# RWKV low-rank mixes on 32 of the 128 rows of TensorE each

## The chip, the cores and the metric

The kernel runs on one core of one Trainium2 chip. The metric is the device time of one execution in microseconds (us), the median of several runs. The engines are TensorE (PE for its matmuls, PEld for its weight loads), VectorE (DVE), ScalarE (ACT), GpSimd (POOL) and the queue that starts DMAs (SP). PSUM is the memory that TensorE writes; it has eight banks of 512 float32 columns on 128 partitions.

## What is computed

The program is a stack of eight residual layers over an input of 32 sequences of 256 tokens with 128 features. Only the first layer, an RWKV-like mixer, is touched by the change. Its beginning, cut from the reference:

```python
shifted = jnp.pad(x, ((0, 0), (1, 0), (0, 0)))[:, :T]
delta = shifted - x
low = jnp.tanh((x + delta * mu_x) @ W_x1).reshape(B, T, 5, PROJ_LR)   # PROJ_LR = 32
mus = jnp.einsum('blnr,dnr->blnd', low, W_x2) + x_bias
xr, xw, xk, xv, xg = [x + delta * mus[:, :, i] for i in range(5)]
r = (xr @ W_r)...; w = (jnp.tanh(xw @ W_w1) @ W_w2 + b_w2)...; k = (xk @ W_k)...
v = (xv @ W_v)...; g = xg @ W_g
```

After that comes a scan over time (S = exp(-exp(w)) * S + k v, per head), a normalisation per head, a gate and an output projection. The five slices of `mus` are the five mixes. Each sums over 32 numbers only.

## The kernel before, in words

The function `stage_rwkv` (from L316) works on 16 groups p of 512 tokens (two sequences). Each group's activations lie with the features on the 128 partitions and the 512 tokens in the free dimension. Everything is float32, and every float32 matmul is recorded as two passes, each with its own weight load.

The low rank of a group is made by two products (`low_rank`, L648 to L653). The first puts columns 0 to 127 of the 160 low-rank columns on the partitions of `low[:, 0]`, the second puts columns 32 to 159 on those of `low[:, 1]`. So the 32 numbers of mix i lie on partitions 32i to 32i+31 of `low[:, 0]` for i = 0 to 3, and on partitions 96 to 127 of `low[:, 1]` for i = 4. The weights `a_wx2` of mix i are laid out on 128 partitions, with zeros on the 96 that do not belong to it. The product of mix i (L565) contracts all 128 partitions; the zeros cancel the rest.

The five products are issued in the order i = 1, 3, 2, 4, 0 (`ORDER`), as j = 0 to 4. They go to PSUM banks 0, 1, 2, 3 and again 0 (`BANK`). So j = 4 must wait until VectorE has read j = 0 out of bank 0 (the wait on `dm_done`). VectorE reads each product with one instruction, `mix_out` (L388), which computes (product + bias) * delta; POOL adds x to three of the five (`add_x`, L516).

Each engine has a list of work written by hand, a loop over g that mixes steps of different groups. The order within one turn is:

- PE: `values(g)` (L553, four products), `mixes(g+1)` (L565, five), `out(g-2)` (L630), `heads(g-1)` (L640, L644), `turn_in(g+2)` (L572, which waits for the residual of VectorE, L456), `decay_low`, `plain_value`, `key`, `decay`, `gate` (L578 to L608), `bonus(g)` (L615), `receptance(g+1)` (L621, L623), `turn_back(g-1)` (L589), `low_rank(g+2)` (L651, L653).
- DVE: `gated(g-2)` (L451), four `outer(g)` (L396), `mix_out` 0 and 1, `scan` 0 (L404), `bonus_key`, `mix_out` 2 to 4, `scan` 1, `residual(g-2)` (L456), `scan` 2 and 3, `variance`, `mix_in(g+2)` (L382), `normalise(g-1)`, `moments(g+3)`, `gate(g+1)`, `bonus_value(g)` (L417).
- ACT: `square`, `evac(g+2)` (L700), `decay_low`, `plain_value`, `root(g-1)` (L691), `key`, `decay`, `gate` (L732), `receptance` (L738), `layernorm(g+3)` (L745), `affine(g-1)` (L715), `low_rank(g+2)` (L757).
- POOL: `add_x`, `read` (L523), `difference` (L511) and `inverse` (L504).

The first turns (g = -3 to -1) fill this pipeline and the last empty it. The two matmuls `decay` (L604) and `bonus` (L615) contract 64 partitions only. In a later layer the product L1142 takes 128 partitions in, but gives 32 columns only, and four heads are put on the four strips of 32 PSUM partitions.

Of the kernel before, what the change touches and what calls it, by code (L numbers as in the profile page):

```python
# [81 lines left out]
def at_least(eng, sem, v):  # L82

    if not (isinstance(v, int) and v <= 0):
        eng.wait_ge(sem, v)
# [193 lines left out]
def stage_rwkv(nc, k, tag, w, x_in, arrive, loads):  # L279
# [5 lines left out]
    with ExitStack() as ctx:  # L285
# [12 lines left out]
        low = sb("low", [P, 2, GW])  # L298
# [38 lines left out]
        at = {name: bank[:, b, :] for name, b in BANK.items()}  # L337
# [206 lines left out]
        def _(pe):  # L544
# [10 lines left out]
            def mixes(p, j):  # L555
                i = ORDER[j]
                if j == 0:
                    pe.wait_ge(s["low_out"], 2 * p + 2)
                elif j == 1:
                    at_least(pe, s["vv_out"], p)  # L560
                elif j == 2:
                    at_least(pe, s["gg_done"], p)
                elif j == 4:
                    pe.wait_ge(s["dm_done"], 5 * p + 1)
                nc.tensor.matmul(at[f"m{j}"], lhsT=w["a_wx2"][:, i, :], rhs=low[:, i // 4, :], start=True, stop=True)\  # L565
                    .then_inc(s["mus_done"], 1)

            def turn_in(p):
# [86 lines left out]
            for g in range(-3, NG + 2):  # L655
                if has(g):
                    for v in range(VQ):
                        values(g, v)
                if has(g + 1):
                    for j in range(5):  # L660
                        mixes(g + 1, j)
                if has(g - 2):
                    out(g - 2)
                if has(g - 1):
                    heads(g - 1)
                if has(g + 2):
                    turn_in(g + 2)
                if has(g + 1):
                    decay_low(g + 1)
                    plain_value(g + 1)  # L670
                    key(g + 1)
                    decay(g + 1)
                    gate(g + 1)
                if has(g):
                    bonus(g)
                if has(g + 1):
                    receptance(g + 1)
                if has(g - 1):
                    turn_back(g - 1)
                if has(g + 2):  # L680
                    low_rank(g + 2)
# [1960 lines left out]
```

## Time and profile before

| What | Value |
|---|---|
| Median of 3 runs | 3591.35 us (3590.38 to 3592.12) |
| The profiled execution's own time | 3593.28 us |
| Its span, first to last instruction | 3591.5 us |
| PE busy (matmuls) | 3117.2 us, 87% |
| PE weight loads | 2057.7 us, 57% |
| DVE busy | 2379.6 us, 66% |
| ACT busy | 1703.2 us, 47% |
| POOL busy | 1203.7 us, 34% |
| Mean granted TensorE clock | 0.905 of full speed |
| Part of the RWKV layer in the span | about 17 to 488 us |

The busy time of PE is that of modelled records: matmuls are pipelined, and a record is longer than the time in which its engine can start the next one. The start of one group to the start of the next is the better measure. A wait in square brackets is the idle time of that engine just before the instruction, with what ended it.

### The profile page before, as it was taken

The page shows a single profiled execution, that of the slowest core. Times are in us where ns is not written, and L with a number is a line of the kernel's source. Part 1 is how long each engine was busy: PE and PEld are TensorE (multiplying, and loading weights), DVE is VectorE, ACT ScalarE, POOL GpSimd, SP SyncE. Part 2 cuts the span into 40 slices and gives each one's busy share as a digit, 9 for nine tenths or more (in the row PEclk, how much of TensorE's full clock was granted, in tenths as well). Part 3 has the DMA queues.
Part 4 walks back from the last instruction along what each step waited for, and adds up shares of the span by engine and source line. Part 5 has one row for each costly group of instructions (what it writes and reads, how often), then busy time and mean ns, then how long its engine had stood idle before and what let it go on. Part 6 is the DMA issues. An engine that isn't in the chain of part 4 may idle for free. (4 is left out here: it accounts for less than half of the span.)

```text
span 3591.5 us, 49433 instructions
## 1 busy us (share of the span) xinstructions
PE 3117.2 (87%) x16500; PEld 2057.7 (57%) x16500; DVE 2379.6 (66%) x5557; ACT 1703.2 (47%) x3659; POOL 1203.7 (34%) x1204
## 2 busy tenths in 40 slices
PE   6999975999872999997589996888989999999989
PEld 2455564888631444444478885677735555555557
DVE  4888875444595777775744445003579999999964
ACT  2443422333231899997133331212446666666644
POOL 3444420000132777775100001001224444444432
PEclk9999967999986999999599995557989999999999
DMA  3000011110032110111111100000000000000001
GB/s 110 1 1 1 1 46 59 39 41 25 26 111 74 29 29 26 29 30 48 53 69 36 45 1 1 0 0 26 1 1 1 1 1 1 1 1 1 1 6 43
DMA packets 106556, 91.24 MB, mean 25 GB/s; under 512 B 15501, under 2 KB 96147, under 8 KB 104000
## 3 DMA queue, kind: packets, MB, share of 16 engines
q1 hardware_dynamic: 104928, 87.25, 7.6%
q8 instruction: 135, 2.21, 0.3%
q14 instruction: 117, 0.96, 0.1%
q10 hardware_dynamic: 1376, 0.82, 0.1%
HBM read 57.60 MB, written 30.15 MB: 24 GB/s over the span
## 5 line engine op out<-in xcount | busy, mean ns | idle before, releaser
L2328 ACT ACTIVATE m_x_hT<-m_x_hid,wm_b 128x260 f32<-128x260 f32 x512 | 242.8, 478 | 433.3 <-PE m_x_hid L2250 433.3
L1326 POOL TENSOR_TENSOR c_tE<-c_tE,c_tDm 128x256 f32<-128x256 f32 x512 | 372.8, 729 | 139.0 <-ACT c_tE L1286 122.3
L1209 DVE TENSOR_REDUCE c_tM<-c_tpa 128x2 f32<-128x512 f32 x512 | 330.0, 681 | 131.2 <-PE c_tpa L1111 130.3
L1286 ACT ACTIVATE c_tE<-c_tpb 128x512 f32<-128x512 f32 x512 | 310.1, 607 | 43.0 <-PE c_tpb L1128 43.0
L2250 PE MATMUL m_x_hid<-m_x_xg,wm_w 128*128 128x260 f32 x1024 | 305.9, 385 | 8.8 <-ACT m_x_hT L2328 5.3
L2258 PE MATMUL m_x_yp<-m_x_hT,wm_w 128*128 128x260 f32 x1024 | 300.6, 383 | 0.0
L1662 POOL TENSOR_TENSOR b_wkv<-b_at,b_rec 128x512 f32<-128x512 f32 x128 | 163.3, 1275 | 306.0 <-DVE b_rec L1598 306.0
L1111 PE MATMUL c_tpa<-c_tK,c_Qm 96*128 96x256 f16 x1024 | 205.1, 283 | 48.8 <-DMA c_Qm<-aug_d 35.6
L79 POOL TENSOR_TENSOR rstd<-vareps,neg_half 128x4 f32<-128x4 f32 x80 | 86.4, 1080 | 460.0 <-DVE vareps L68 460.0
L2175 DVE TENSOR_SCALAR m_x_yT<-m_x_yp,wm_b 128x260 f32<-128x260 f32 x128 | 62.5, 489 | 253.4 <-PE m_x_yp L2258 253.4
L1128 PE MATMUL c_tpb<-c_Qm,c_tK 101*128 101x256 f16 x1024 | 198.5, 275 | 23.5 <-ACT c_tE L1286 23.4
L1267 ACT ACTIVATE c_tDm<-wc_pos,c_LD 128x128 f32<-128x128 f32 x512 | 209.1, 411 | 19.9 <-PEq L93 19.9
L2258 PEld LDWEIGHTS m_x_yp<-m_x_hT,wm_w 128*128 128x128 f32 x1024 | 193.8, 190 | 29.4
L2250 PEld LDWEIGHTS m_x_hid<-m_x_xg,wm_w 128*128 128x128 f32 x1024 | 182.8, 190 | 42.3 <-ACT m_x_hT L2328 15.8
L1656 POOL TENSOR_TENSOR b_dt<-b_er,b_bt 128x512 f32<-128x512 f32 x128 | 163.5, 1277 | 129.9 <-DVE b_er L1582 96.7
L2145 POOL TENSOR_TENSOR m_x_xl<-m_x_xs,m_x_xh 128x1024 f16<-128x1024 f32 x16 | 34.2, 2140 | 467.6 <-ACT m_x_xh L2317 467.6
L2433 PE MATMUL r_rec<-r_ring,wr_a 128*128 128x32 f32 x512 | 150.8, 388 | 42.3 <-ACT r_ring L2479 42.3
L72 DVE TENSOR_SCALAR xn<-X,mean,rstd 128x128 f32<-128x128 f32 x320 | 128.5, 462 | 84.6 <-POOL rstd L79 83.0
L2433 PEld LDWEIGHTS r_rec<-r_ring,wr_a 128*128 128x128 f32 x512 | 129.2, 312 | 66.1 <-ACT r_ring L2479 65.4
L1111 PEld LDWEIGHTS c_tpa<-c_tK,c_Qm 96*128 96x128 f16 x1024 | 70.4, 98 | 167.5 <-DVE c_tM L1209 88.6
L2291 PE MATMUL m_x_misc<-m_x_ys,m_x_sel 104*128 104x128 f32 x1280 | 151.9, 276 | 4.2 <-DVE m_x_ys L2190 4.2
L2291 PEld LDWEIGHTS m_x_misc<-m_x_ys,m_x_sel 104*128 104x128 f32 x1280 | 146.6, 192 | 7.7 <-DVE m_x_ys L2190 7.7
(322 smaller groups left out, 7363.2 us busy)
## 6 DMA issues: line engine op xcount, KB each, us to landing
m_x_ir<-idx_d SPq DMA_DIRECT2D x16, 1040.0 KB, 6.8
xn_d<-xn SPq DMA_DIRECT2D x32, 256.0 KB, 2.3
m_x_xs<-xn_d SPq DMA_DIRECT2D x16, 512.0 KB, 4.1
c_tK<-k_d SPq DMA_DIRECT2D x32, 192.0 KB
c_Qm<-q_d SPq DMA_DIRECT2D x128, 48.0 KB
wm_w<-in_m_w SPq DMA_DIRECT2D x2, 2048.0 KB, 9.5
gate_d<-c_pgate SPq DMA_DIRECT2D x16, 256.0 KB
q_d<-c_phi SPq DMA_DIRECT2D x32, 128.0 KB
```

What stands on the lines that cost most here:

```text
L1111: m = nc.tensor.matmul(pa[:, h % 2, qt, :], lhsT=Qm[0:QROWS, u, h, qt * P:(qt + 1) * P], rhs=K[0:QROWS, u, h // HG, :], start=True, stop=T ...
L1128: m = nc.tensor.matmul(pb[:, h % 2, kt * T:(kt + 1) * T], lhsT=K[:, u, h // HG, kt * P:(kt + 1) * P], rhs=Qm[:, u, h, :], start=True, stop ...
L1209: nc.vector.tensor_reduce(out=M[:, u % 2, 2 * h:2 * h + 2], in_=pa[:, h % 2], axis=AX.X, op=ALU.max).then_inc(s["max_done"], 1)
L1267: nc.scalar.activation(Dm[:, u % 2, h, :], w["c_pos"][:], ACT.Exp, scale=LD[:, bass.ds(b * HB + h, 1)]).then_inc(s["dexp"], 1)
L1286: nc.scalar.activation(E[:, h % 8].rearrange("p a q -> p (a q)"), pb[:, h % 2, :], ACT.Exp).then_inc(s["exp_done"], 1)
L1326: nc.gpsimd.tensor_tensor(diag, diag, Dm[:, u % 2, h:h + 1, :].to_broadcast([P, 2, P]), ALU.mult).then_inc(s["dmul_done"], 1)
L1656: nc.gpsimd.tensor_tensor(dt_[:, m % 2, :], er[:, m % 4, :], bt[:, m % 2, :], ALU.add).then_inc(s["d_done"], 1)
L2250: nc.tensor.matmul(hid[:, c % 2, 0:QW], lhsT=w["m_w1"][:, e, j * P:(j + 1) * P], rhs=xg[:, slot, e, :, :].rearrange("p b c -> p (b c)"), s ...
L2258: mm = nc.tensor.matmul(yp[:, e % 2, 0:QW], lhsT=w["m_w2"][:, e, j, :], rhs=hT[:, e % 2, j, :], start=(j == 0), stop=(j == NJH - 1))
L2291: mm = nc.tensor.matmul(misc[:, bank, h * D:(h + 1) * D], lhsT=sel[:, b, c, h * P:(h + 1) * P], rhs=ys[:, b % 2, c, :], start=(c == 0), st ...
L2328: nc.scalar.activation(hT[:, e % 2, j, :], hid[:, c % 2, 0:QW], ACT.Gelu, bias=w["m_b1"][:, c:c + 1]).then_inc(s["gelu_done"], 1)
L2433: nc.tensor.matmul(rec[:, c % 2, t * B:(t + 1) * B], lhsT=w["r_a"][:], rhs=prev, start=False, stop=True, skip_group_check=True).then_inc(s ...
```

## The change

The product of each mix takes the 32 rows that hold its numbers, of the weights and of the low rank. For i = 4 these are rows 96 to 127, as for i = 3. Nothing else changes: the order, the banks, the waits, the number of instructions and of semaphore increments stay.

```diff
--- before.py
+++ after.py
@@ -562,7 +562,8 @@
                     at_least(pe, s["gg_done"], p)
                 elif j == 4:
                     pe.wait_ge(s["dm_done"], 5 * p + 1)
-                nc.tensor.matmul(at[f"m{j}"], lhsT=w["a_wx2"][:, i, :], rhs=low[:, i // 4, :], start=True, stop=True)\
+                rows = slice(32 * min(i, 3), 32 * min(i, 3) + 32)
+                nc.tensor.matmul(at[f"m{j}"], lhsT=w["a_wx2"][rows, i, :], rhs=low[rows, i // 4, :], start=True, stop=True)\
                     .then_inc(s["mus_done"], 1)
```

## Rows read from the trace of the kernel before

**Rows 1.** Stretch: length; busy (records) of PE, PEld, DVE, ACT, POOL; clock, DMA.

```profile
200.00:400.00 200.00, 185.25 (x725) 102.01 (x726) 170.79 (x295) 89.09 (x152) 93.05 (x74) 1.00 0.00 1
```

**Rows 2.** Order of time, steady turns: start, us, engine, line, operation, count, [idle before].

```profile
241.31 0.69 DVE L451 TENSOR_TENSOR a_z<-a_nt,a_gg 128x512 f32<-128x512 f32 x1 [2.56 <-ACT a_nt L715]
...
268.31 0.69 DVE L451 TENSOR_TENSOR a_z<-a_nt,a_gg 128x512 f32<-128x512 f32 x1 [2.56 <-ACT a_nt L715]
...
271.48 4.45 PE L565 MATMUL a_bank<-a_low,wa_wx 128*128 128x512 f32 x10
...
272.54 1.61 DVE L388 SCALAR_TENSOR_TENSOR a_xi<-a_bank,wa_xb,a_delta 128x512 f32<-128x512 f32 x2 [0.17 <-PE a_bank L565]
...
275.77 1.05 PE L630 MATMUL a_bank<-wa_wo,a_z 128*128 128x128 f32 x8
...
277.37 2.05 DVE L388 SCALAR_TENSOR_TENSOR a_xi<-a_bank,wa_xb,a_delta 128x512 f32<-128x512 f32 x3
...
282.31 0.63 PE L572 MATMUL a_bank<-ident,xn 128*128 128x128 f32 x4 [1.02 <-DVE X L456]
...
295.86 0.69 DVE L451 TENSOR_TENSOR a_z<-a_nt,a_gg 128x512 f32<-128x512 f32 x1 [2.56 <-ACT a_nt L715]
```

**Rows 3.** Waits summed over 130 to 430 us: total us, times, longest.

```profile
DVE a_z L451 <- ACT a_nt L715: 28.7, 12, 2.6
...
PE a_bank L572 <- DVE X L456: 7.9, 11, 1.0
...
DVE a_xi L388 <- PE a_bank L565: 1.8, 11, 0.2
```

**Rows 4.** Order of time, second half of a turn, 259 to 266 us.

```profile
259.10 1.12 PE L604 MATMUL a_bank<-a_tw,wa_ww 64*128 64x512 f32 x2
...
260.15 1.12 PE L608 MATMUL a_bank<-a_xi,wa_wg 128*128 128x512 f32 x2
...
261.21 1.12 PE L615 MATMUL a_bank<-a_ruk,wa_csel 64*128 64x512 f32 x2
...
265.90 1.10 PE L651 MATMUL a_bank<-a_xm,wa_wx 128*128 128x512 f32 x2 [1.21 <-DVE a_cv L417]
```

**Rows 5.** Order of time, PE, a product on four column strips, 1303 to 1305 us.

```profile
1303.67 1.07 PE L1142 MATMUL c_tpv<-c_tE,c_tVs 128*32 128x256 f32 x16
1304.68 0.39 PE L1111 MATMUL c_tpa<-c_tK,c_Qm 96*128 96x256 f16 x2
```

**Rows 6.** Order of time, the filling of the pipeline, 32 to 50 us.

```profile
32.82 6.22 PE L565 MATMUL a_bank<-a_low,wa_wx 128*128 128x512 f32 x10 [1.84 <-ACT a_low L757]
...
38.87 0.60 PE L572 MATMUL a_bank<-ident,xn 128*128 128x128 f32 x4
```

```profile
34.93 0.75 DVE L388 SCALAR_TENSOR_TENSOR a_xi<-a_bank,wa_xb,a_delta 128x512 f32<-128x512 f32 x1 [6.18 <-PE a_bank L565]
36.50 3.32 DVE L388 SCALAR_TENSOR_TENSOR a_xi<-a_bank,wa_xb,a_delta 128x512 f32<-128x512 f32 x4 [0.81 <-PE a_bank L565]
49.70 0.69 DVE L396 TENSOR_TENSOR a_kv<-a_vp,a_kk 128x512 f32<-128x512 f32 x1 [2.80 <-PE a_vp L553]
```

**Rows 7.** Order of time, PE, behind the last turn with mixes, 455 us.

```profile
454.60 1.96 PE L553 MATMUL a_vp<-a_xi,wa_wv 128*128 128x512 f32 x4 [1.27 <-ACT a_rr L738]
```

**Rows 8.** Order of time, PE, matmuls behind idle gaps, 100 to 1036 us.

```profile
100.75 1.76 PE L651 MATMUL a_bank<-a_xm,wa_wx 128*128 128x512 f32 x2 [2.15 <-DVE a_cv L417]
...
979.70 3.67 PE L935 MATMUL c_pqk<-c_pxT,wc_wqk 128*128 128x512 f32 x8 [2.32 <-DVE c_pcs L851]
...
998.36 5.37 PE L935 MATMUL c_pqk<-c_pxT,wc_wqk 128*128 128x512 f32 x8 [2.04 <-DVE c_pcs L851]
1007.68 3.67 PE L935 MATMUL c_pqk<-c_pxT,wc_wqk 128*128 128x512 f32 x8 [1.77 <-DVE c_pcs L851]
...
1035.66 5.37 PE L935 MATMUL c_pqk<-c_pxT,wc_wqk 128*128 128x512 f32 x8 [1.92 <-DVE c_pcs L851]
```

**Rows 9.** Granted TensorE clock, stretch 102 to 104 us.

```profile
102.00:104.00 2.00, 2.00 (x3) 0.50 0.00 0
```

## Prediction

> **What bounds the kernel now.** I first read the busy time by stretch. In the middle of the RWKV layer PE looks fullest, 185 of 200 us, with DVE at 171 [rows 1]. Those PE records are modelled and overlap, so this does not say that PE is the limit. The order of time and the waits decide. One turn takes 27.0 or 27.55 us in alternation (L451 at 241.31, 268.31 and 295.86). In its first half the five mixes start at 271.48 and the next work on PE (L630) at 275.77: ten passes in 4.29 us, 0.43 us a pass, 0.86 us a mix [rows 2]. Behind them PE does the output and the heads, and then stands still: the transposes L572 wait 1.02 us for VectorE's residual [rows 2]. That wait comes once a turn, 7.9 us in 11 turns, longest 1.0 [rows 3]; with five or six of 1.02, the rest are about 0.45 us, in step with the two lengths of the turn. In the second half PE stands still again, 1.21 us in front of L651, for DVE's `cv` [rows 4]. DVE has one large wait, 2.56 us in front of L451 for ACT's L715, the end of a chain DVE moments, POOL, ACT layernorm, ACT affine; 28.7 us in 12 times [rows 3]. No mix is in it. For the mixes DVE waits only 0.17 us a turn, 1.8 us in 11 [rows 3]. So the steady turn is bound by DVE with its round trip over POOL and ACT, and PE has slack behind the mixes.
>
> **What the change does to the mixes.** Their order in row strips is 1, 3, 2, 3, 0. The first three have strips and banks of their own; the fourth needs the strip of the second; the fifth waits for bank 0. So at most three, not four, start at once. Whether strips really run together no row of before shows for rows. For columns it does: 16 float32 passes of 256 columns of L1142 fill only 1303.67 to 1304.68, 1.01 us [rows 5], where passes one after the other at half of 0.43 would take 16 x 0.215 = 3.4 us. I take the same for row strips. The other bound is no overlap at all, 0.86 us a mix.
>
> Entering and leaving the 32-row shape costs something. The two 64-row products and the 128-row product between them follow each other at 1.05 and 1.06 us [rows 4] instead of 0.86: 0.19 us whenever the number of rows changes. I charge 0.19 at entry and 0.19 at exit; the bounds are nothing, and 0.19 at each of the five mixes.
>
> **Steady turn, 15 of them (mixes of groups 1 to 15).** Mix 0 comes 0.19 us later, so `mix_out` 0 starts at 272.73 instead of 272.54. Before, the second `mix_out` waited for mix 1: the pair took 1.61 us [rows 2], while three in a row take 2.05, 0.68 each. Now mix 1 is ready with mix 0, and the pair takes about 1.42 us: it ends at 274.15 as before. The 0.19 paid at entry is given back there. Net 0 us. Bounds: 0.17 + 0.19 = 0.36 a turn gained if entry were free, 5.4 us; and 0.38 a turn lost if nothing overlaps and each mix pays 0.19, 15 x 0.38 = 5.7 us.
>
> On PE the block shrinks: entry 0.19, mixes 0 to 2 0.86, mix 3 0.86 more, mix 4 from 273.5 (after `mix_out` 0) to 274.4, exit 0.19: L630 starts at about 274.6 instead of 275.77, 1.2 us earlier. Output and heads move with it, and DVE, which reads the output just before L572, does not reach that residual sooner. So the 1.2 us become idle time before L572: gaps of about 2.2 and 1.65 us in place of 1.02 and 0.45. What is late next is unchanged: `residual`, then the ACT chain. The last turn with mixes has no L572, and PE has no gap to lose the time in; but L553 after it waits 1.27 us for ACT [rows 7], whose list runs `key`, `decay`, `gate` and `receptance` behind the `root` that needs DVE's variance. Gain 0; at best the 1.2 us.
>
> **Filling, group 0.** Here PE does bind. The mixes start at 32.82 and L572 follows at 38.87, 6.05 us, the first passes slow (first `mix_out` only at 34.93), then PE has no idle time to the first `kv` at 49.70, which waited 2.80 us for it [rows 6]. A slow mix is 2 x 0.86 = 1.72 us. With strips: mixes 0 to 2 to 34.5, mix 3 to 36.3, mix 4 partly at the faster rate to 37.0, exit 0.19: L572 at 37.2, 1.65 us earlier. DVE follows: its first `mix_out` is unchanged at 34.93, the other four start without the 0.81 us wait and end at about 38.3 instead of 39.82. Nothing but PE lies between here and 49.70, so 1.6 us are gained. Bounds: 0 and 2.4 (four of five mixes at the same time).
>
> The Trainium skill ("TensorE: Matmul & The Clock Gate", Measured speedup vs the span model) gives 3.07 times for four row strips of 32. By it three slow mixes together would take somewhat longer than one, and the filling would gain some 0.3 us less (an estimate from that page). The column strips of this trace come to 3.4 [rows 5], and the sum goes by them. The same page (The mechanism) has matmuls start in strict program order. Then the two passes of a mix would hold back the next mix by one pass, and three mixes would end one pass apart; by that the steady sum stays (DVE takes 0.68 us for each, a pass is 0.43) and the filling gains 0.1 us less. Whether this holds for row strips no run here shows.
>
> **TensorE's clock.** The new gap of 2.2 us is the one risk. After 2.15 us of idle time before L651 at 100.75 [rows 8] the granted clock went to 0.50, that is 1.2 in place of 2.4 GHz [rows 9]. L935 shows both outcomes: behind gaps of 2.04 and 1.92 us its eight passes took 5.37 us, behind 2.32 and 1.77 us 3.67 us [rows 8]. So three of four gaps of 1.9 to 2.4 us were followed by a slow stretch which cost 1.7 us of PE time (5.37 - 3.67), and gaps of 1.77 or less by none. Of the waits for the residual (groups 4 to 15, twelve) six would be 2.2 us long. I take three falls, bounds 0 and 12. The price of one: PE is 1.7 us later in the second half of a turn. PE has 1.21 us of slack before L651 [rows 4], so 1.7 - 1.21 = 0.5 us is the least, and 1.7 the most. Between them lies what ACT hands on: its `key`, `decay` and `gate` wait for PE one after the other, and DVE's `gate` and `cv` for them. I take 0.7, near the lower end, since most of the lateness meets that slack: 3 x 0.7 = 2.1 us.
>
> **The sum.** -1.6 (filling) + 0 (steady) + 2.1 (clock) = +0.5 us. Against the profiled execution's 3593.28 us (span 3591.5 and 1.8 around it) that is 3593.8. The median of the runs lies 1.9 us below that execution, so the forecast is 3591.35 + 0.5, 3591.8 us: no change that can be told. About 0.2%, 7.2 us, is what a measurement of this kernel can tell from no change.
>
> **Rivals.**
> (a) No overlap. The strips run one after the other, each with 0.19 us: the change does not do what it says. For it: the sharing was only seen for columns, where all strips go to one bank; here each writes all 128 partitions. Against it: the banks and strips differ. Time: 15 x 0.38 = 5.7 plus about 1.0 in the filling, +6.7: 3598.0. Chance 0.11, half of it above 7.2 us.
> (b) The clock falls in nearly every turn. The place is the gap before L572, the price 0.7 to 1.7 us for each, and it decides from about 8 falls on. Half the gaps are only 1.65 us, which speaks against it; that a lower activity of 32 rows may count as idle speaks for it. Twelve falls at 1.1 give 13 us, less 1.6: 3602.8. Chance 0.08.
> (c) The clock never falls and the entry is free: -1.6 - 5.4 = -7.0, 3584.4. Against it are rows 4. Chance 0.08, a third of it below -7.2.
> (d) Another length of the turn. The two lengths differ by 0.5 us because DVE's scans and POOL's adds slow each other; the new start of the adds could settle on either: six turns x 0.5 = 3 us either way, 3588 or 3595. This is still "same"; it has 0.15.
> The forecast's own case, with zero to six falls, has the remaining 0.58, from 3589.8 to 3594.
>
> **How the numbers follow.** The range reaches to (a) and (d) and lets go of (b) and most of (c): 3587.0 to 3598.0, nine tenths by my chances less what I distrust them. Slower by over 0.2%: half of (a) and nearly all of (b), 0.12. Faster by over 0.2%: a third of (c), 0.03. Same: 0.85.
>
> **What would show it.** In the profile after: the ten L565 records of a steady turn within about 3 us instead of 4.45 and starting in threes; L388's first pair in 1.4 us with a wait of about 0.36 before it; L630 at 3.1 us after the first mix instead of 4.29; the wait of L572 for X near 2.2 and 1.6 us; L572 of the filling at 37.2, and `kv` at 48.1. The granted clock of the windows between 105 and 430 us shows the falls. The prediction is wrong if mixes follow each other at 0.86 us or more, if the wait of L388 exceeds 0.4 us, or if the turn is no longer 27.0 and 27.55 us with the clock at 1.00.

## The result and the profile after

The changed kernel takes 3598.11 us (median of 12 runs, 3596.27 to 3603.22), the kernel before 3592.2 us in 12 runs on the same chip (3590.38 to 3594.22). The ratio is 1.0018 with a 95% interval of 1.001 to 1.0027: 6 us slower in the middle, between 3.6 and 9.7. The forecast was 3591.8, no change, with a range up to 3598.0, just short of this. The profiled execution took 3598.12 us, its span 3596.2, 4.7 more than before.

**A steady turn.** The timeline of the kernel after, all engines. The diff adds a line, so L565 of before is L566 now, L572 is L573, L630 is L631, L715 is L716.

```profile
244.38 0.69 DVE L451 TENSOR_TENSOR a_z<-a_nt,a_gg 128x512 f32<-128x512 f32 x1 [2.56 <-ACT a_nt L716]
...
271.57 0.69 DVE L451 TENSOR_TENSOR a_z<-a_nt,a_gg 128x512 f32<-128x512 f32 x1 [2.55 <-ACT a_nt L716]
...
274.84 3.08 PE L566 MATMUL a_bank<-a_low,wa_wx 32*128 32x512 f32 x10
...
276.00 1.41 DVE L388 SCALAR_TENSOR_TENSOR a_xi<-a_bank,wa_xb,a_delta 128x512 f32<-128x512 f32 x2 [0.36 <-PE a_bank L566]
...
276.82 2.88 POOL L516 TENSOR_TENSOR a_xi<-a_xi,a_xT 128x512 f32<-128x512 f32 x2 [7.63 <-DVE a_xi L388]
...
277.32 2.93 DVE L404 TENSOR_TENSOR_SCAN a_S<-a_dec,a_kv 128x256 f32<-128x256 f32 x2
...
277.85 1.16 PE L631 MATMUL a_bank<-wa_wo,a_z 128*128 128x128 f32 x8
...
285.75 0.63 PE L573 MATMUL a_bank<-ident,xn 128*128 128x128 f32 x4 [2.28 <-DVE X L456]
...
299.31 0.69 DVE L451 TENSOR_TENSOR a_z<-a_nt,a_gg 128x512 f32<-128x512 f32 x1 [2.56 <-ACT a_nt L716]
```

Against [rows 2]: the block of mixes is as short as the prediction said (L631 follows the first mix by 3.01 us instead of 4.29), the wait of L388 is 0.36 and its pair takes 1.41. All that was gained on PE is idle time in front of L573, 2.28 us instead of 1.02. But the turns are 27.19 and 27.74 us, not 27.0 and 27.55. The next two lines are the same place in the kernel before.

```profile
273.37 2.88 POOL L516 TENSOR_TENSOR a_xi<-a_xi,a_xT 128x512 f32<-128x512 f32 x2 [7.44 <-DVE a_xi L388]
...
274.07 2.73 DVE L404 TENSOR_TENSOR_SCAN a_S<-a_dec,a_kv 128x256 f32<-128x256 f32 x2
```

The scan (L404) starts 5.76 us behind L451 in the kernel before (its L451 is at 268.31 [rows 2]) and 5.75 behind it after. It then takes 2.73 us before and 2.93 after. What did move is POOL: its add starts 5.06 us behind L451 before and 5.25 after, 0.50 instead of 0.70 us ahead of the scan, and so lies beside more of it.

**Whether strips overlap.** A window of 0.3 us at the start of the mixes after, PE alone: the first passes of three mixes run within the time of one.

```profile
274.84 0.71 PE L566 MATMUL a_bank<-a_low,wa_wx 32*128 32x512 f32 x3
```

The three start within 14 ns of each other, then come their three second passes.

**The waits from 130 to 430 us after**: idle time in all, count, longest.

```profile
DVE a_z L451 <- ACT a_nt L716: 27.4, 11, 2.6
...
PE a_bank L573 <- DVE X L456: 18.5, 10, 2.3
...
DVE a_xi L388 <- PE a_bank L566: 4.0, 11, 0.4
```

Against [rows 3], the wait for the residual has grown from 7.9 to 18.5 us, that of L388 from 1.8 to 4.0, and the one that binds the turn, L451 on ACT, is there as before.

**Filling, after.** PE first, then DVE.

```profile
32.60 4.99 PE L566 MATMUL a_bank<-a_low,wa_wx 32*128 32x512 f32 x10 [1.83 <-ACT a_low L758]
37.51 1.12 PE L573 MATMUL a_bank<-ident,xn 128*128 128x128 f32 x4
38.56 1.97 PE L579 MATMUL a_vp<-a_xi,wa_ww 128*64 128x512 f32 x2
...
50.52 0.69 DVE L396 TENSOR_TENSOR a_kv<-a_vp,a_kk 128x512 f32<-128x512 f32 x1 [2.80 <-PE a_vp L553]
```

L573 follows the first mix by 4.91 us instead of 6.05 [rows 6]. Yet L579 still ran at 0.98 us a pass, the slow rate, and the first `kv` came 17.92 us behind the first mix, against 16.88 before. The 1.14 us gained in the block were lost behind it, and 1.0 more: the granted clock rose to 1.00 at 42.0 us, where it had risen at 36.2 before.

**The clock.** Windows of the kernel after: stretch, length, busy PE (records), granted clock.

```profile
165.00:168.00 3.00, 3.00 (x11) 1.00 0.00 0
168.50:171.70 3.20, 3.20 (x17) 0.50 0.00 0
394.00:397.00 3.00, 1.40 (x6) 1.00 0.00 0
397.20:400.40 3.20, 3.20 (x7) 0.50 0.00 0
```

Between 105 and 430 us the clock fell to 0.50 four times (at 120.5, 141.0, 168.3 and 397.0), before not once. Two of the falls (120.5 and 397.0) came as foreseen, behind a gap of some 2.28 us before L573; the window from 394 shows PE half idle. The other two came with PE busy throughout, right behind the 32-row mixes. This is the timeline of PE around the one at 168.3:

```profile
161.12 3.95 PE L553 MATMUL a_vp<-a_xi,wa_wv 128*128 128x512 f32 x8
165.00 3.09 PE L566 MATMUL a_bank<-a_low,wa_wx 32*128 32x512 f32 x10
168.02 1.82 PE L631 MATMUL a_bank<-wa_wo,a_z 128*128 128x128 f32 x8
```

Behind these two falls L573 waits less for VectorE. These are its next instructions after the falls at 141.0 and 168.3; their neighbours wait 1.74 and 2.28 us.

```profile
148.19 0.63 PE L573 MATMUL a_bank<-ident,xn 128*128 128x128 f32 x4
...
175.91 0.63 PE L573 MATMUL a_bank<-ident,xn 128*128 128x128 f32 x4 [0.64 <-DVE X L456]
```

**Where the 4.7 us lie.** From the first L451 (103.17 before, 103.38 after) to the last (486.72 and 492.23) the kernel after takes 5.3 us more. Thirteen turns pay about 0.19, 2.5 us. Most of the other 2.8 lies in four turns, counted beyond their 0.19: 1.66 in the first (30.91 us instead of 29.06), 0.27 in the second (27.45 instead of 26.99), 0.45 in that of 397.0 (28.17 instead of 27.53) and 0.13 in the one behind it (24.60 instead of 24.28). The first turn holds the fall at 120.5 and a low stretch at 100.1 that lasts 6.8 us, where before it was 3.4. The second turn holds the fall at 141.0, but its 0.27 come from the fall in the turn ahead of it: its mixes already start late, and gap_only (below) has the same 0.27 there with no fall in that turn. So the two falls with PE busy cost nothing (the turn of 168.3 takes 27.72 against 27.54, the 0.19), since idle time before L573 takes them up. The fall at 397.0, behind a gap, cost 0.58 in its two turns. Ahead of it all are 0.2 us more, behind it 0.8 less, which changes as much from one execution to the next.

### The profile page after: what moved, and what is told of

The parts are those of the page before. It is cut to its first block and busy times, and to the rows that moved or that the text cites. A ratio compares the mean times of both kernels' runs of the same rounds, so it can differ in the third digit from the quotient of the medians.

```text
span 3596.2 us, 49433 instructions
## 1 busy us (share of the span) xinstructions
PE 3109.5 (86%) x16500; PEld 2045.7 (57%) x16500; DVE 2381.8 (66%) x5557; ACT 1701.6 (47%) x3659; POOL 1202.3 (33%) x1204
```

## The experiments

Two theories about the clock: the longer gap alone makes it fall, or the work in 32 rows does. Two about the turn: DVE is late through PE's entry into the new shape, or through POOL beside the scan. All ratios are to the kernel before on the same chip. "Falls" are those between 105 and 430 us in the profiled execution.

**group0_full.** Group 0 keeps full rows, the others have strips.

```diff
+                rows = slice(32 * min(i, 3), 32 * min(i, 3) + 32) if p else slice(0, P)
```

> The changed kernel, but the mixes of group 0 alone contract all 128 rows again. Theory clock: in the filling of the pipeline the products on 32 rows left the clock low until about 42 us (before: 36 us); with full rows it rises near 36 us again, the first L396 starts about 0.8 us earlier than the 50.5 of the changed kernel (49.7), L566 to L573 takes 6.05 us again, and the total is 0 to 1 us below the changed kernel's 3598.1. Rival: the filling's loss comes from something else in the stage (loads, alignment); then the first L396 stays at 50.5 and the total does not move. Steady turns stay 27.19 and 27.73 us by both.

Measured: 1.0012 (1.0002 to 1.0021), median 3599.96 us, turns 27.20 and 27.73, three falls. PE in the filling:

```profile
32.32 6.26 PE L566 MATMUL a_bank<-a_low,wa_wx 128*128 128x512 f32 x10 [2.21 <-ACT a_low L758]
38.41 0.60 PE L573 MATMUL a_bank<-ident,xn 128*128 128x128 f32 x4
38.94 1.07 PE L579 MATMUL a_vp<-a_xi,wa_ww 128*64 128x512 f32 x2
```

The block is long again (6.09 us to L573), but the clock is up right behind it, and `kv` comes 16.92 us behind the first mix. So strips in group 0 gave no gain; what decides there is when the clock rises. All profiles of the experiments say the same. With five mixes on 32-row strips in group 0 the clock was up for good at 42.0, 41.3, 41.9, 41.2 and 41.7 us (after, after_again, filler, after_short_add, order_strips) and in one_strip, without overlap, at 45.7. With full rows it was up at 36.2, 36.4, 35.7, 37.1 and 36.9 (before, group0_full, gap_only, before_short_add, order_full). In first2_full and half_rows it was up ahead of the first mix, at 31.4 and 31.6; they say nothing on this, but show what the rate is worth: `kv` came 13.9 us behind the first mix in both.

**filler.** The strips stay, and three products of 128 rows go in front of the output, to fill PE's gap. Their results are written over.

```diff
+                for _ in range(3):
+                    nc.tensor.matmul(at["y"][:, 0:T], lhsT=w["a_wo"][:], rhs=z[:, 0:T], start=True, stop=True,
+                                     skip_group_check=True)
```

> The changed kernel, with three extra products of 256 columns (0.43 us each, 1.3 us together, all 128 rows) in front of the output projection L631; they write the bank that the projection overwrites. They give PE back the 1.2 us that the strips saved. Theory gap: the new falls of the clock come from the longer idle time before L573 (2.28 and 1.74 us); with the filler it is 1.0 and 0.45 us again and no fall but those of the kernel before (near 70 and 101 us) is left; total 1 to 2.5 us below 3598.1. Rival rows: the falls follow the products on 32 rows themselves, since two of them (at 141 and 168 us) came with no idle time before; then falls at the start of the output projection or soon behind the mixes remain, some of them, and the total moves by less than 1 us. Steady turns 27.19 and 27.73 by both.

Measured: 1.002 (1.001 to 1.0029), turns 27.2 and 27.73. The wait for the residual is nearly as short as before, 6.2 us in the stretch (--lines view: busy, mean ns, idle before). The clock fell all the same, at 250.1 and 277.4, behind the mixes.

```profile
L573 PE MATMUL a_bank<-ident,xn 128*128 128x128 f32 x44 | 6.9, 278 | 6.2 <-DVE X L456 6.2
```

```profile
246.00:251.00 5.00, 5.00 (x16) 0.91 0.00 0
251.00:254.00 3.00, 3.00 (x14) 0.59 0.00 0
```

PE is busy for all of both windows. The gap is not the only cause, and filling it gives nothing back in the total.

**one_strip.** All mixes take rows 0 to 31, so the shape is entered as in the kernel after but nothing overlaps. The numbers computed differ.

```diff
+                rows = slice(0, 32)
```

> The changed kernel, but all five mixes read rows 0 to 31 of weights and low rank, so no two can share the array (mixes 1 to 4 are computed from other rows than theirs). Theory (entry and overlap): the five follow each other at 0.86 us, mix 0 is 0.19 us late as in the changed kernel, the pair of L388 takes about 1.6 us and not 1.41, and the turn grows by another 0.19 us to 27.4 and 27.9 us; L631 starts 4.5 us behind the first mix; total about 3600 to 3602. Rival: overlap is of no use to the time, and the turn stays at 27.19 and 27.73, total 3598. If single products on 32 rows left alone lower the clock, there are as many falls as in the changed kernel or more.

Measured: 1.0035 (1.0022 to 1.0047), 3607.5 us. The timeline around one block of mixes, in the turn whose L451 starts at 136.47:

```profile
139.73 4.55 PE L566 MATMUL a_bank<-a_low,wa_wx 32*128 32x512 f32 x10
...
140.89 1.61 DVE L388 SCALAR_TENSOR_TENSOR a_xi<-a_bank,wa_xb,a_delta 128x512 f32<-128x512 f32 x2 [0.36 <-PE a_bank L566]
...
141.72 2.52 POOL L516 TENSOR_TENSOR a_xi<-a_xi,a_xT 128x512 f32<-128x512 f32 x2 [7.63 <-DVE a_xi L388]
...
142.41 2.38 DVE L404 TENSOR_TENSOR_SCAN a_S<-a_dec,a_kv 128x256 f32<-128x256 f32 x2
...
144.21 1.63 PE L631 MATMUL a_bank<-wa_wo,a_z 128*128 128x128 f32 x8
```

Without overlap the block is 4.48 us again. L388 still waits 0.36, and now its pair takes 1.61 as before. The scan therefore starts later, 5.94 us behind L451. Yet the pair of scans ends 8.32 us behind L451, just as in the short turns of the kernel after, where it starts at 5.75 (before: start 5.75, end 8.13). POOL's add starts at 5.25 in both. So the end of the scans goes with the start of POOL's add, and not with their own start. The short turn was expected to grow to 27.4 us; it takes 27.19, as in the kernel after. Of the 12 us in the total 5.3 lie ahead of the first L451 (108.49 us instead of 103.17), where PE binds. The clock fell ten times, in nearly every turn, and always with PE busy (the wait for the residual is 0.8 us in the whole stretch):

```profile
138.80:143.00 4.20, 4.20 (x11) 1.00 0.00 0
145.40:148.60 3.20, 3.20 (x19) 0.57 0.02 5
```

The turns take 27.19 and 27.94 us, the longer ones 0.2 more than after. The fall inside them is not the reason, since the one turn of the stretch without a fall takes 27.98. Their L451 waits 2.1 to 2.2 us instead of 2.56, the mark of a fall in the turn ahead (see gap_only). With 4.5 us of 32-row work in a row the clock came down ten times, with 3.0 us of it twice in the kernel after.

**first2_full.** Mixes 0 and 1 keep full rows, the last three take strips. The entry now lies where DVE isn't waiting.

```diff
+                rows = slice(32 * min(i, 3), 32 * min(i, 3) + 32) if j > 1 else slice(0, P)
```

> The changed kernel, but the first two mixes contract all 128 rows again and only the last three use strips. Theory entry: the turn is longer by 0.19 us because the change of the row count exposes the load of mix 0 in front of the first L388; with the entry moved behind mix 1, L388 waits 0.17 us again, its pair takes 1.61 us, and the turn is back at 27.0 and 27.54 us; total 2 to 3 us below 3598.1, and not below 3591 (falls of the clock remain). Rival: the turn is longer because products in several banks at once, or POOL's adds, slow VectorE; then it stays above 27.1 and 27.6 us.

Measured: 1.0005 (0.9996 to 1.0015), turns 27.0 and 27.53, no fall.

```profile
268.24 1.61 DVE L388 SCALAR_TENSOR_TENSOR a_xi<-a_bank,wa_xb,a_delta 128x512 f32<-128x512 f32 x2 [0.17 <-PE a_bank L566]
269.77 2.73 DVE L404 TENSOR_TENSOR_SCAN a_S<-a_dec,a_kv 128x256 f32<-128x256 f32 x2
270.10 1.16 PE L631 MATMUL a_bank<-wa_wo,a_z 128*128 128x128 f32 x8
```

The wait is 0.17, the scan 2.73, the turn that of before, though L631 follows the first mix by 2.92 us and the wait for the residual is longer than after (21.8 us in 11). It is the entry in front of mix 0 that lengthens the turn, and a gap of 2.3 us does not always bring the clock down.

**before_short_add and after_short_add.** To see whether the 0.19 us reach the turn through POOL, the first two of POOL's three adds (the inputs of decay and value) work on 8 columns of each sequence; the rest of those sums is left out.

```diff
+                xs, xo = (seq(xi[:, i, :]), x(p)) if j == 3 else (seq(xi[:, i, :])[:, :, 0:8], x(p)[:, :, 0:8])
+                nc.gpsimd.tensor_tensor(xs, xs, xo, ALU.add).then_inc(s["xi_done"], 1)
```

> The kernel before, with the first two of POOL's three adds of x cut to 8 columns of each sequence (so most of the x term of the decay and value inputs is left out). It is the partner of the next run. The first scan no longer meets long adds: the two scan instructions behind the first pair of L388 take about 2.05 us together in every turn, where they took 2.38 and 2.73 us. The two lengths of the turn should come together.

> The changed kernel with the same two adds cut to 8 columns. Theory pool: the entry's 0.19 us is paid back by the pair of L388 (1.41 in place of 1.61 us), so the first scan starts when it did, but POOL's adds start 0.19 us later, lie longer beside the scan and stretch it by 0.19 us; with short adds the scan takes the same time in both kernels and the turn is within 0.05 us of that of before_short_add. Rival: the strips themselves slow VectorE's scan (PE writes three banks at once); then the scan and the turn stay 0.15 to 0.2 us longer than in before_short_add.

Measured, a single execution each: 3576.07 and 3573.31 us, too few to compare their totals. The turns are 25.88 and 26.07 us in the one, 25.88 and 26.06 in the other. The scan, from 130 to 430 us: busy, mean ns of one. First the kernel before with short adds, then the kernel after with them, then after as it is.

```profile
L404 DVE TENSOR_TENSOR_SCAN a_S<-a_dec,a_kv 128x256 f32<-128x256 f32 x96 | 92.4, 1010 | 0.0
```

```profile
L388 DVE SCALAR_TENSOR_TENSOR a_xi<-a_bank,wa_xb,a_delta 128x512 f32<-128x512 f32 x60 | 41.5, 739 | 4.3 <-PE a_bank L567 4.3
...
L404 DVE TENSOR_TENSOR_SCAN a_S<-a_dec,a_kv 128x256 f32<-128x256 f32 x96 | 92.4, 1010 | 0.0
```

```profile
L404 DVE TENSOR_TENSOR_SCAN a_S<-a_dec,a_kv 128x256 f32<-128x256 f32 x88 | 100.8, 1192 | 0.0
```

L388 waits 0.36 us as with long adds (4.3 in 12 turns), but with POOL gone from beside the scan the turn no longer feels it. In the kernel before the mean is 1167 ns: 88 scans by 25 ns are 2.2 us in 11 turns, 0.2 a turn. That is the whole loss of the steady turn. The first pair of scans takes less than the 2.05 us expected; this is the kernel before with short adds:

```profile
261.54 1.26 DVE L404 TENSOR_TENSOR_SCAN a_S<-a_dec,a_kv 128x256 f32<-128x256 f32 x2
```

Beside the long adds it takes 2.38 and 2.73 us, in the short and the long turn. The difference is the 1.1 and 1.5 us by which the turns are shorter here: what these two adds cost VectorE in this layer is some 17 us (3576.07 in one execution against 3592.93, the median before on this chip), as much as the reordered lists below give.

**gap_only.** From the kernel before: the fourth and the fifth product (i = 4 and 0) take all rows but only 128 of the 512 columns; the rest of these two mixes is not computed. PE gets its gap with no 32-row work at all.

```diff
+                cols = P if j > 2 else GW
+                nc.tensor.matmul(at[f"m{j}"][:, 0:cols], lhsT=w["a_wx2"][:, i, :], rhs=low[:, i // 4, 0:cols], start=True, stop=True)\
```

> The kernel before, all mixes on 128 rows, but the fourth and the fifth product compute only 128 of their 512 columns (the rest of those two mixes keeps what the bank held). That takes about 1.3 us off PE in front of L630 and makes the wait of L572 for VectorE about 2.3 and 1.7 us, as in the changed kernel, with no product on 32 rows and no entry. Theory rows: the new falls of the clock follow the work on 32 rows, so with the idle time alone no fall is added between 110 and 440 us, turns stay 27.0 and 27.54 us, total within 1 us of before. Rival gap: the idle time alone makes the clock fall, some of the twelve waits are followed by a fall, and those turns are 0.4 to 0.7 us longer.

Measured: 1.0004 (0.9995 to 1.0014), turns 27.0 and 27.54 with the clock at 1.00, and two falls, at 117.6 and 172.2. Timeline and windows around the first:

```profile
117.15 0.69 PE L573 MATMUL a_bank<-ident,xn 128*128 128x128 f32 x4 [2.28 <-DVE X L456]
```

```profile
116.00:118.00 2.00, 0.85 (x5) 0.90 0.00 0
118.00:121.00 3.00, 3.00 (x4) 0.50 0.00 0
```

So the clock can fall at a gap of 2.28 us with no 32-row work near; the theory that only the rows matter falls too. There are two causes. This run also shows what a fall behind a gap leaves to the next turn. The turn between these two starts holds no fall, but takes 27.26 us instead of 26.99, and its L451 waits 2.14 instead of 2.56: VectorE came late to it.

```profile
131.10 0.69 DVE L451 TENSOR_TENSOR a_z<-a_nt,a_gg 128x512 f32<-128x512 f32 x1 [2.14 <-ACT a_nt L716]
...
158.36 0.69 DVE L451 TENSOR_TENSOR a_z<-a_nt,a_gg 128x512 f32<-128x512 f32 x1 [2.56 <-ACT a_nt L716]
```

The fall at 172.2 costs 0.58 us in its turn and the next (27.85 and 27.27).

**half_rows.** Strips of 64 rows, two at once. Zeros of the weights cancel the rows that do not belong to the mix, so the products are the same.

```diff
+                rows = slice(64 * (i > 1), 64 * (i > 1) + 64)
```

> The changed kernel with strips of 64 rows: mixes 0 and 1 on rows 0 to 63, mixes 2, 3 and 4 on rows 64 to 127 (the zeros of the weights cancel the rest). Theory entry: the row count still changes, so L388 waits 0.36 us and the turn is 27.19 and 27.73 us; two products at a time, so L631 starts between 3.0 and 3.9 us behind the first mix. Theory rows for the clock: with twice the rows there are fewer falls behind the mixes than in the changed kernel. Rival: turns at 27.0 and 27.54 us, since 64 rows cost no entry.

Measured: 1.001 (1.0 to 1.0019), turns 27.19 and 27.73, two falls (117.0, 393.5), both behind a gap.

```profile
271.28 3.09 PE L566 MATMUL a_bank<-a_low,wa_wx 64*128 64x512 f32 x10
272.44 1.41 DVE L388 SCALAR_TENSOR_TENSOR a_xi<-a_bank,wa_xb,a_delta 128x512 f32<-128x512 f32 x2 [0.36 <-PE a_bank L566]
```

Leaving the 128-row shape costs the same with 64 rows. No fall with PE busy was seen in this execution; as the kernel after has only one or two of them, one profile does not show that they are gone.

**after_again.** The kernel after, unchanged, for the spread of filling and clock.

> The changed kernel once more, for a second profile of it. The turn without a fall is 27.19 and 27.73 us again (entry), while the number and places of the falls between 105 and 455 us need not be the same: 2 to 6 are expected. Total 1.0010 to 1.0027 of before.

Measured: 1.0019 (1.0009 to 1.0028), turns 27.19 and 27.73, three falls (119.8, 167.6, 396.3), at the places of the first profile but for 141.0. The first `kv` came 16.64 us behind the first mix (17.92 in the first profile). With the same code the filling varies by 1.3 us, as much as the strips save in the block.

**order_full, order_strips, order_last3.** All of the above says that what sets the turn is not PE's time, but when DVE gets its inputs. So `affine(g - 1)` moves in front of `layernorm(g + 3)` in ACT's list, and `low_rank(g + 1)` between the values and ahead of the mixes in PE's. The first is made from the kernel before, the second from the kernel after, the third with strips for the last three mixes alone.

```diff
@@ PE
-                    for v in range(VQ):
-                        values(g, v)
+                    values(g, 0)
+                    values(g, 1)
+                if has(g + 1):
+                    low_rank(g + 1)
+                if has(g):
+                    values(g, 2)
+                    values(g, 3)
...
-                if has(g + 2):
-                    low_rank(g + 2)
@@ ACT, in front of layernorm(g + 3) instead of behind it
+                if has(g - 1):
+                    affine(g - 1)
```

> The kernel before (mixes on 128 rows) with two lists reordered: ACT runs affine in front of the layernorm of the group three ahead, and PE puts the two low-rank products behind the first two value products. It takes away the 2.56 us wait of VectorE's L451 and the 1.2 us of PE in front of L651. Theory bound: the steady turn was set by that round trip and not by the mixes, so the turn falls from 27.0 and 27.5 us to about 25, total 3592 - 15 x 2 = about 3562. Rival: PE was the limit after all; then the turn falls by less than 0.5 us.

> The changed kernel (mixes on strips) with the same two lists reordered. Theory bound: with the round trip gone PE is nearly always busy, and now the 1.2 us that the strips save on it are worth something: the turn is 0.4 to 1.0 us shorter than in order_full, total 5 to 12 us below order_full. Rival: VectorE sets the turn in both, the 0.19 us of the entry is all that the strips do, and order_strips is 1 to 5 us slower than order_full (falls of the clock included).

> The reordered lists of order_full with strips for the last three mixes only. Theory: the entry lies behind mix 1 and costs nothing, the turn without a fall is 25.77 and 26.30 us as in order_full; what PE saves is idle time before L573. A fall of the clock costs 1.5 us a turn here, as in order_strips; with fewer than there the total lies 0 to 6 us above order_full. Rival: the shorter PE block is worth something in this order, total 1 to 3 us below order_full.

Measured: order_full 0.9955 (0.9938 to 0.9971), 3575.49 us, turns 25.77 and 26.30, no fall. It is 16 us faster than the kernel before (by the interval 10 to 22). The turn was expected at 25 us and the total at 3562; it is less, since the next wait stands in the place of the old one, `kv` on PE's values:

```profile
252.22 0.68 DVE L451 TENSOR_TENSOR a_z<-a_nt,a_gg 128x512 f32<-128x512 f32 x1
...
256.14 0.69 DVE L396 TENSOR_TENSOR a_kv<-a_vp,a_kk 128x512 f32<-128x512 f32 x1 [1.88 <-PE a_vp L553]
```

order_strips 0.9982 (0.9972 to 0.9991), turns 26.03 and 26.50 (0.2 more) and five falls; order_last3 0.9961 (0.9947 to 0.9976), turns 25.77 and 26.30 and four falls. The strips were expected to take 5 to 12 us off the better order; order_strips is 11 us slower by the medians (3586.54 and 3575.49), and order_last3 can't be told from order_full. In the shorter turn a fall behind a gap costs 1.5 us (28.05 instead of 26.50) where it cost 0.45; the one fall of order_strips with PE busy, at 188.5, cost nothing here too (25.95). This is order_strips, the gap before one of the falls:

```profile
276.17 0.63 PE L573 MATMUL a_bank<-ident,xn 128*128 128x128 f32 x4 [2.28 <-DVE X L456]
```

The strips do not help the better order either; the full rows are the better choice in both orders.

## Why the prediction was wrong

**What bounds the turn: right.** The PE time saved turned into idle time in front of L573 and into nothing else, and L451's wait for ACT stayed.

**The mixes on PE: right.** Ten passes in 3.08 us, starting in threes, L631 at 3.01 us (forecast 3.1). The sharing seen for columns [rows 5] holds for rows. The prediction took from the Trainium skill's "The mechanism" ("TensorE: Matmul & The Clock Gate"), by which matmuls start in strict program order, that the mixes might end a pass apart. The trace agrees with the order of the mixes, which start 7 ns after each other, but not with what was made of it: three first passes start within 14 ns and the second passes follow.

**The entry's price: right.** The 0.19 us come as taken from [rows 4], with 32 rows and with 64.

**The steady turn: wrong. This step failed:** "The 0.19 paid at entry is given back there. Net 0 us." DVE does get it back: the scan starts 5.75 us behind L451 as before. But the step followed only DVE. Between mix and scan the first `mix_out` also releases POOL, 0.19 us later, and the scan beside POOL's add ends 0.2 us later, whether it starts at 5.75 (after) or at 5.94 us (one_strip). The runs: 27.19 for 27.0 with the entry in front of mix 0 (after, filler, half_rows), 27.0 with it behind mix 1 (first2_full), and no difference with short adds. It costs 2.5 us in the span. The prediction's own sign of being wrong, a turn that is no longer 27.0 and 27.55 us with the clock at 1.00, came true. My rival (d) named the contention, but as a jump of 0.5 us in either direction.

**The filling: wrong.** The step was "Nothing but PE lies between here and 49.70, so 1.6 us are gained". It took the clock's rise as unchanged. The block gave 1.14 us, but the slow rate lasted to 42.0 us instead of 36.2, and the first L451 came 0.2 us later than before. That the clock rises late with 32-row mixes is seen in all six profiles that have them in all of group 0, and in none of the five with full rows. How this comes about stays open.

**The clock: the price right, a term missing.** Three falls at 0.7 us were 2.1. There were two behind gaps, of six gaps of 2.28 us: 0.58 for the one at 397.0, and about 0.7 for the one at 120.5 (estimated from filler, which has no fall there: its first turn takes 30.48 us, 0.43 less than after, and 0.27 in the next turn). Two more came with PE busy and cost nothing. The rest is the low stretch at 100 us, of 6.8 instead of 3.4 us, which the sum did not have at all: filler has it too, and its first turn is 1.2 us above 29.06 and the entry. Whether the strips make it longer stays open: gap_only and half_rows have it as well, first2_full and group0_full do not. I had put the cause in the gap alone: gap_only shows that it is a cause, filler and one_strip that the 32-row work is another, with PE never idle. Rival (b) had that remark ("a lower activity of 32 rows may count as idle"), with 0.08.

**The sum.** -1.6, 0 and +2.1 gave +0.5. Measured in the span: +0.2 (all ahead of the first L451), +2.5, +2.8 and -0.8 behind the layer, 4.7 in all. So the steady turn is the largest miss with 2.5, the filling the next with 1.8, and the clock was off by 0.7. The medians differ by 6; the other 1.3 us lie within the ratio's interval and are put down to nothing. The total is that of rival (a), but not by its mechanism: the strips do overlap.

## What to carry to other kernels

A product made smaller on an engine that is not the bound can still cost: follow what its first consumer releases on every engine, down to what then runs beside what. Row strips made PE's block 1.3 us shorter here and nothing faster, since PE did not bind; no run here shows a gain from them. If you take them, place the change of shape where nobody waits for the first product, and count the clock as a cost: it fell both at the idle time that they make and behind the 32-row work itself. Ask what POOL does beside a scan of VectorE: two of its adds cost 1.1 to 1.5 us a turn. Where DVE waits for a chain over other engines, look at the order of their lists first: here that was worth 16 us.

## What was not expected of the hardware

- The clock fell from 1.00 to 0.50 with PE busy without a pause, behind 3.0 us of 32-row products in groups of three (twice after, twice in filler, once each in after_again, group0_full, after_short_add and order_strips) and in nearly every turn behind 4.5 us of them one after the other (ten times). With full rows (before, gap_only, order_full, before_short_add) it never fell so between 105 and 430 us.
- Gaps of 2.28 us have different outcomes: six of them in gap_only between 105 and 430 us brought two falls, six in first2_full none.
- float32 products with two passes each, on strips and banks of their own, start their first passes within 14 ns, and then their second.
- A pair of scans 128x256 takes 1.26 us beside short adds and, in the kernel before, 2.38 or 2.73 us beside POOL's adds of 128x512. It ends 0.2 us later when the add starts 0.2 us later, whether its own start moves (one_strip) or not (after).
